# GpSimd compares the up weights with their threshold block by block, and three magnitudes of the down weights move into the first heads

## The reference

```
def ternarize_weights(w):
    gamma = jnp.mean(jnp.abs(w))
    return jnp.sign(jnp.round(w / (gamma + EPS))) * gamma
h = bitlinear(x, w_fc)             # 512 -> 2048, layer norm and quantised x
h = jax.nn.gelu(h, approximate=False)
return bitlinear(h, w_proj)        # 2048 -> 512
```

## Time and profile before

| | before |
|---|---|
| median of 3 runs | 1260.82 us |
| the profiled execution | 1258.53 us, span 1256.8 us |
| TensorE busy in the span | 1156.8 us (92%) |
| VectorE busy | 972.4 us (77%) |
| ScalarE busy | 770.1 us (61%) |
| GpSimd busy | 592.8 us (47%) |
| mean granted TensorE clock | 0.977 of full speed |

### The profile page before, as it was taken

One profiled execution on the slowest core, in us unless ns is written; L12 is line 12 of the kernel. 1 busy time (PEld: TensorE's weight loads), 2 busy tenths in 40 slices (PEclk: granted clock), 3 DMA queues, 4 the chain that ended last, 5 costly groups with the idle time before them and its releaser, 6 DMA issues.

```text
span 1256.8 us, 24649 instructions
## 1 busy us (share of the span) xinstructions
PE 1156.8 (92%) x9204; PEld 634.7 (51%) x9204; DVE 972.4 (77%) x2862; ACT 770.1 (61%) x1430; POOL 592.8 (47%) x658
## 2 busy tenths in 40 slices
PE   6968799999999999999999999999999999987997
PEld 4434444555445554555445554555545554554443
DVE  5988778688787878779796888779786887868634
ACT  5568747675566646675476655766466755577480
POOL 2143216941398125961279314971369412981260
PEclk9978899999999999999999999999999999997999
DMA  9441220123111230121310231112301221001000
GB/s 347 106 159 38 73 59 9 27 60 95 49 36 27 66 112 4 33 60 35 109 25 17 68 89 43 35 33 62 110 5 31 61 80 30 3 2 45 16 9 34
DMA packets 75514, 72.37 MB, mean 58 GB/s; under 512 B 34721, under 2 KB 60289, under 8 KB 74243
## 3 DMA queue, kind: packets, MB, share of 16 engines
q1 hardware_dynamic: 75395, 70.79, 20.1%
HBM read 29.63 MB, written 8.39 MB: 30 GB/s over the span
## 4 chain that ended last, share of the span: by engine, by line
PE 51%; DVE 30%; ACT 11%; issue 3%; POOL 3%; DMA 2%; SPq 1%; POOLq 0%; ACTq 0%; DVEq 0%
PE gen L511 17%; PE down L559 16%; DVE score L1229 8%; PE pv L626 5%; DVE hT L1106 4%; PE score L587 4%; DVE probs L1106 2%; PE gen L578 2%; ACT probs L918 1%; POOL rstd L1620 1%; DVE qkn L1336 1%; DVE bn L1260 1%; DVE mx L1229 1%; DMA x2T<-b_proj 1%; DVE gen L1229 1%
## 5 line engine op out<-in xcount | busy, mean ns | idle before, releaser
L1620 POOL TENSOR_TENSOR rstd<-veps,mhalf 128x1 f32<-128x1 f32 (+1 forms) x104 | 67.0, 644 | 460.5 <-DVE veps L1309 312.4
L918 ACT ACTIVATE probs<-score 128x512 f16<-128x512 f32 x360 | 189.8, 527 | 102.4 <-PE score L602 102.4
L511 PE MATMUL gen<-x2T,t1T 128*128 128x512 f16 x1024 | 240.1, 379 | 3.3 <-ACT x2T L838 1.8
L1106 DVE TENSOR_TENSOR probs<-score,probs 128x512 f16<-128x512 f32 x360 | 199.5, 595 | 45.1 <-ACT score L920 44.0
L559 PE MATMUL down<-t2T,hT 128*128 128x512 f16 x960 | 221.1, 382 | 0.0
L920 ACT ACTIVATE score<-score 128x512 f32<-128x512 f32 x360 | 192.5, 535 | 0.0
L511 PE MATMUL gen<-xT,wa 128*128 128x512 f16 x672 | 156.0, 382 | 4.2 <-DVE mx L1229 3.7
L1106 DVE TENSOR_TENSOR hT<-gen,hT 128x512 f16<-128x512 f32 x156 | 105.8, 685 | 68.6 <-ACT gen L866 34.5
L511 PEld LDWEIGHTS gen<-x2T,t1T 128*128 128x128 f16 x1024 | 95.5, 97 | 107.3 <-ACT x2T L838 4.5
L1229 DVE CUSTOM_DVE_ANT_0 score<-score,mask_rows 128x512 f32<-128x512 f32 (+3 forms) x312 | 143.0, 520 | 0.0
L559 PEld LDWEIGHTS down<-t2T,hT 128*128 128x128 f16 x960 | 90.3, 98 | 98.5 <-issue 2.7
(11 more groups left out here) (190 smaller groups left out, 1822.7 us busy)
## 6 DMA issues: line engine op xcount, KB each, us to landing
qk<-qkn SPq DMA_DIRECT2D x360, 64.0 KB, 2.0
xo<-x SPq DMA_DIRECT2D x8, 1024.0 KB, 5.7
out<-xn SPq DMA_DIRECT2D x31, 256.0 KB, 2.2
hT<-x SPq DMA_DIRECT2D x7, 1024.0 KB, 6.3
hT<-w_fc SPq DMA_DIRECT2D x4, 1024.0 KB, 16.2
hT<-w_down SPq DMA_DIRECT2D x4, 1024.0 KB, 5.2
t2T<-w_qk SPq DMA_DIRECT2D x4, 512.0 KB, 7.4
probs<-w_v SPq DMA_DIRECT2D x1, 1024.0 KB, 10.3
```

The lines of the kernel that those rows point to most:

```text
L511: mm = nc.tensor.matmul(bank[:, :], a, b, start=(start and n == 0), stop=(stop and n == len(pairs) - 1))
L918: nc.scalar.activation(probs[:, h % 2, HI, 512 * i:512 * i + n], bank[:, 0:n], ACT.Exp, scale=1.0 / S_UP)
L1106: return V.tensor_tensor(out, whole, hi, ALU.subtract)
```

## The change

GpSimd compares each block of the up weights with theta itself, in place, and then multiplies it; VectorE's four `large(0, i)` go. GpSimd waits for theta (`g_step` at 2) and, between comparing and multiplying a block, for its own semaphore `large_block`. Of the four magnitudes of w_down the first stays at the end of ScalarE's lead-in; the others follow at heads 0, 2 and 4. The total and threshold of w_down move from head 2 to head 5, VectorE's `large(1, i)` from heads 3, 4, 5, 6 to 5, 7, 9, 11, and ScalarE's scaling from heads 4 to 9 to heads 7 to 12. Lines of the changed kernel are 2 or 3 further down than the same lines before.

```diff
--- before.py
+++ after.py
@@ -45,13 +45,15 @@
 
 
 PIECES = EC
-LARGE_AT = {3: 0, 4: 1, 5: 2, 6: 3}
+LARGE_AT = {5: 0, 7: 1, 9: 2, 11: 3}
+MAGNITUDE_AT = {0: 1, 2: 2, 4: 3}
+THRESHOLD_AT = 5
 
 
 USUAL_STEP_MAX = {8: 0, 9: 1, 10: 2, 11: 3, 12: 4, 13: 5}
 FIRST_STEP_MAX = {6: 0, 8: 1, 9: 2, 10: 3, 12: 4, 14: 5}
 EARLY = len(USUAL_STEP_MAX)
-SCALED = range(4, 10)
+SCALED = range(7, 13)
 MAX_AT = {0: 6, 2: 7, 3: 8, 5: 9, 7: 10, 8: 11, 9: 12, 10: 13, 11: 14, 12: 15}
 SHIFT_AT = 14
 
@@ -279,6 +281,7 @@
         wv_hi, wv_low, wp_hi, rot_hi = (sem(n) for n in ("wv_hi", "wv_low", "wp_hi", "rot_hi"))
         w_ready = sem("w_ready")
         p_step = sem("p_step")
+        large_block = sem("large_block")
         g_sums, g_step, g_total, sign_ready, large_ready, tern_ready = (
             sem(n) for n in ("g_sums", "g_step", "g_total", "sign_ready", "large_ready", "tern_ready"))
         c_full, c_ready = sem("c_full"), sem("c_ready")
@@ -795,7 +798,7 @@
                             scores(h + 1)
                         elif nxt:
                             values(0)
-                        if setup and h == 2:
+                        if setup and h == THRESHOLD_AT:
                             gamma_total(1)
                         if nxt and h in STEP_MAX:
                             max_pass(STEP_MAX[h], 1, in_general=True)
@@ -1027,8 +1030,7 @@
                     queries_keys(3, 1)
                     for tb in range(TB):
                         values(tb)
-                    for i in range(3):
-                        magnitudes(1, wdown_in, i)
+                    magnitudes(1, wdown_in, 0)
                     return
 
                 if setup:
@@ -1062,8 +1064,8 @@
                         exponents(h + 1)
                     if setup and h - 1 in SCALED:
                         scaled(h - 1)
-                    if setup and h == 0:
-                        magnitudes(1, wdown_in, PIECES - 1)
+                    if setup and h in MAGNITUDE_AT:
+                        magnitudes(1, wdown_in, MAGNITUDE_AT[h])
                     if prev and here and h in FINISH_AT:
                         final(FINISH_AT[h])
                 if here:
@@ -1447,20 +1449,16 @@
                     qk_low(3, 1)
                     maxima(6, 1)
                     thresholds(0)
-                    large(0, 0)
                     v_low(0)
                     maxima(7, 1, in_general=True)
                     v_low(1)
                     maxima(8, 1)
-                    large(0, 1)
                     v_low(2)
                     maxima(9, 1, in_general=True)
                     v_low(3)
                     maxima(10, 1)
-                    large(0, 2)
                     maxima(11, 1, in_general=True)
                     maxima(12, 1)
-                    large(0, 3)
                     for h in range(13, HEADS):
                         maxima(h, 1, in_general=(h % 2 == 1))
                     return
@@ -1653,8 +1651,12 @@
                     m, b = divmod(n, FC)
                     flat = t2_flat if m else t1_flat
                     cols = slice(E * b, E * (b + 1))
-                    if b % (FC // PIECES) == 0:
-                        pool.wait_ge(large_ready, n // (FC // PIECES) + 1)
+                    if m == 0:
+                        pool.wait_ge(g_step, 2)
+                        P.tensor_scalar(stage[:, cols], stage[:, cols], theta[:, 0:1], None, ALU.is_gt).then_inc(large_block, 1)
+                        pool.wait_ge(large_block, b + 1)
+                    elif b % (FC // PIECES) == 0:
+                        pool.wait_ge(large_ready, b // (FC // PIECES) + 1)
                     P.tensor_tensor(flat[:, cols], flat[:, cols], stage[:, cols], ALU.mult).then_inc(tern_ready, 1)
 
                 def finish(tb):
```

## The result

| | before | after |
|---|---|---|
| median | 1260.89 us (4 runs, 1259.26 to 1261.31) | 1284.2 us (4 runs, 1281.67 to 1284.85) |
| ratio after / before, 95% interval | | 1.0182 (1.0166 to 1.0198) |
| the profiled execution | 1258.53 us, span 1256.8 us | 1284.85 us, span 1283.1 us |

What follows compares the result with a forecast made beforehand. It took ScalarE's lead-in and, about as late, the shift rows queued behind w_down's loads to bound the first head. Head 0's start +4.1 and the heads +2.2 made +6.3 us, stated as 1267.1, range 1260.5 to 1276.

Steps and rivals of the forecast that it cites:

- The price of GpSimd's comparison: GpSimd's up weights in the lead-in: 0.64 us a compare, 1.85 a block, sixteen blocks 29.6, ending at 87.4.
- a compare over 0.9: Stated sign of a wrong prediction: GpSimd's comparison of one block takes more than 0.9 us.
- The queue: SyncE's queue before head 0: shift rows leave behind w_down's fourth load, which waits for GpSimd; first scores +4.9 us.
- The landing: Shift rows before the first scores: they land 5.5 us after GpSimd's end, delayed by the load's data; otherwise 3.1.
- the forecast 92.9: Start of the first scores in head 0, put at 92.9 us instead of 88.08.
- The first exponents: ScalarE in head 0: exponents start 0.96 us after the scores instead of 1.78, so −0.8.
- Two more magnitudes: ScalarE in heads 2 and 4: 7.8 us added, 5.6 of it hidden in idle time, so +2.2.
- VectorE's lead-in: VectorE without its four wide compares before head 0: halved shift ready about 5.7 us earlier, at 78.1.
- The things costed at nothing: Later threshold and total, wide compares of w_down and output scaling among the heads: taken to cost 0.
- The slow compare: Rival, chance 0.27: GpSimd's compare costs 1.04 to 1.27 us like two-read operations, total 1273.5 to 1277.2.
- The cover: Rival, chance 0.13: shift rows land 3.1 after GpSimd's end, two magnitudes wholly hidden; +1.7, 1262.5 us.
- keep its clock: Rival, chance 0.10: TensorE's granted clock stays up in the heads, −6.9 us; with early landing −3.0, 1257.8.

Runs made afterwards that it cites:

- shift_first: The changed kernel with the two shift transfers ahead of the third and fourth load of w_down: 1262.95 us, ratio 1.0028.
- shift_fourth: The changed kernel with the two shift transfers ahead of the fourth load of w_down only: 1271.02 us, ratio 1.0089.
- shift_second: The changed kernel with the two shift transfers right behind the first load of w_down: 1257.54 us, ratio 0.9980.
- compare_only: The kernel before with only the comparison of the up weights moved to GpSimd: 1278.49 us, ratio 1.0148.
- heads_only: The changed kernel with the comparison of the up weights put back on VectorE: 1262.65 us, ratio 1.0028.
- larges_apart: As `shift_second`, with VectorE's wide compares of w_down at heads 6, 7, 10, 12 instead of 5, 7, 9, 11: 1259.78 us, ratio 0.9999.
- down_compare: As `shift_second`, with GpSimd also comparing three of the four pieces of w_down, VectorE keeping one at head 5: 1258.26 us, ratio 0.9984.

## Why the prediction was wrong

The sign, the road and the place were right; one price was not. Point by point:

- **The price of GpSimd's comparison** is the step that failed: "I take 0.64, because it is the same count of columns, one read, a comparison". It took 1.59 in the mean, and lay outside the stated bounds as well, whose upper end (1.27, adding two tensors) rested on the thought that an operation with one input can't cost more than one with two. The runs put in its place that at this size the kind of instruction decides: tensor with number 1.49 to 1.57, product of two tensors 1.16, copy 0.61. The prediction had named a compare over 0.9 as a sign that it was wrong. In the sum: GpSimd started 0.36 later than reckoned and its 16 blocks took 103.32 − 58.20 = 45.1 instead of 29.6, 15.5 more. The Trainium skill (GPSIMD Engine Reference, section 4.1 on engine selection), which calls elementwise work with one input on this engine roughly line-rate, is borne out by the copy at most (0.61); the measured 1.49 to 1.57 of the other one-input rows speak against it.
- **The queue** was right: first scores wait for the shift rows, these for four loads, these for GpSimd, and the three kernels of the change with other orders show it. The landing was 109.34 − 103.32 = 6.0 after GpSimd's end, forecast 5.5. The shift rows took 4.5 to 5.0 us to land behind a load that was issued just before (4.8 in the change, 4.5 in `shift_first`, 5.0 in `shift_fourth`) and 2.1 in `shift_second`, where the load was 12 us older. With the ring order of the Trainium skill (DMA: Bandwidth & Descriptors, section on queues, rings and completion order) this agrees. So the first scores are 0.36 + 15.5 + 0.5 = 16.4 us later than the forecast 92.9.
- **The first exponents**, −0.8: right.
- **Two more magnitudes**, forecast +2.2: measured +4.2 on the heads against before and +2.0 against `compare_only`. I let all of ScalarE's 5.6 us of idle time hide them; 3.6 of it did against before. Between the two stands the granted clock of one step of the heads, 1.00 in before and 0.75 in `compare_only`, which was in no term. So whether this term was too small stays open; `heads_only`, with 81.07, has the longer heads without the comparison, but does not separate the two.
- **VectorE's lead-in.** I reckoned the shift rows 5.7 us earlier, at 78.1; they were ready at 81.33 against 83.84, 2.5 earlier. Of the 3.2 us that are missing, 1.9 are waits of VectorE for ScalarE's copies of the values, which the wide compares had filled before, 0.3 a later theta (57.95), and 0.4 VectorE's last product (0.69 instead of 0.28). It hung on nothing here, but it is what `shift_second` gets.
- **The things costed at nothing.** The wide compares cost nothing that `larges_apart` or `down_compare` could tell. Threshold and scaling were not tried by themselves, and one wait did grow with the threshold's move: at head 5 TensorE stands 3.28 us for the sums of the magnitudes (0.58 before, at head 2). TensorE in order of time, after:

```profile
140.86 0.59 PE L495 MATMUL down<-gt,ones 128*128 128x1 f32 x2 [3.28 <-DVE gt L1171]
```

ScalarE was at the last magnitude meanwhile, and then waited 0.19 us for TensorE's scores; whether the rest of the wait costs anything is not shown.
- **The rivals.** The slow compare was the true case, with a price still too low: it went to 1277.2. With 1.59 its own rule gives 16 × 0.95 = 15.2 more than the forecast, 1282.3; with the heads' 2.0 it is 1284.3, near the measured 1284.2. That it is so near is in part luck: GpSimd's later start and slower blocks, the landing and the rest of the program, 0.4 + 0.3 + 0.5 + 1.6 = 2.8 us, are left out, and the profiled executions make up for it (below). The cover did not hold. TensorE did not keep its clock: in the 27 and 40 us behind the first scores after was granted 0.83 and 0.83, before 0.93 and 0.79.

In the profiled executions the change cost 26.3 us where the sum said 6.3: the 20.0 between them are 16.4 at the first scores, 2.0 in the heads and 1.6 in the rest of the program, which was in no term. The medians say 17, because the profiled execution of before lay 2.3 below its median, which the forecast had added, and that of after 0.7 above.

## What to carry to other kernels

Before work moves to an engine, time that very instruction there, on the tile's size. Neither the nearest row by inputs (0.64) nor the dearest row at hand (1.27) was a bound for it here, and a miss of 0.95 us became 15 us by being done sixteen times in a row. In a queue that keeps its order, ask of every transfer what it waits for and who waits for what stands behind it; a small urgent transfer belongs ahead of a large one whose buffer comes free late, unless that one is urgent too, as the third load was in the kernel before. A gain at the start (4.1 us earlier first scores in `shift_second`) is worth only what the work moved out of the way does not take back where it lands (3.6 us). And compare short stretches with more than one trace: heads with the same instructions took 77.5 to 79.3 us.

## What was not expected of the hardware

A tensor-with-number instruction on GpSimd, 128x512, takes 1.49 to 1.57 us and the product of two tensors 1.16, as shown above.

Where one GpSimd comparison took 2.00 instead of 1.56 (at 83.40), VectorE had this instruction, which took 0.68 before; VectorE in order of time, after:

```profile
82.43 1.53 DVE L1148 SCALAR_TENSOR_TENSOR p_bias<-x2T,p_bias 1x512 f16<-1x512 f32 x1
```

Both are long where they overlap, and not by chance: in all eight kernels in which GpSimd compares at that time the pair took 1.99 to 2.00 and 1.52 to 1.53 us, in before and `heads_only`, where GpSimd has nothing to do then, VectorE's took 0.68. That the one holds up the other fits this; how was not tried. It is 0.4 us of GpSimd's time here.

The rest of the program, from the turn of outputs on, has the same instructions in all kernels and yet took 1088.4 (`compare_only`) to 1093.0 us (`shift_first`). The kernels agree within 0.7 us up to the last batch's shift; the spread lies in the last 157 to 161 us and goes with the granted clock: in the 40 us behind the last shift it was 1.00 in the two shortest (156.9 and 157.0), 0.91 in the three longest (160.6 to 161.5) and 0.96 in the seven between. The 40 us behind the last shift, by stretch as in the earlier trace rows, in after (last stretch 161.4 us):

```profile
1121.70:1161.70 40.00, 35.73 (x357) 21.33 (x355) 28.09 (x63) 28.32 (x60) 30.25 (x29) 0.91 0.03 9
```

and in `compare_only` (156.9 us):

```profile
1119.80:1159.80 40.00, 34.23 (x386) 21.04 (x383) 28.94 (x68) 30.30 (x65) 30.40 (x29) 1.00 0.03 9
```

At 1.00 TensorE got through more matmuls in less busy time. What decides which clock a run is granted there stays open; it is worth some 4 us, as much as the smaller effects of this study, which is why their intervals are given.
